# A Mamba block and a routed FFN on one core: x_proj rows split later, expert units in other slots, last part reordered, conv in slot 2 and delta's matmul in slot 3

## The reference

```python
# mixer: hidden = ctx (4, 1024, 512), z = layernorm(x) over (B, DI, L)
x  = einsum('ed,bld->bel', in_proj_w, hidden)
u  = silu(causal depthwise conv, 4 taps, of x + conv_b)
x_dbl = einsum('ke,bel->bkl', x_proj_w, u)        # 32 rows dt, 16 B, 16 C
delta = softplus(dt_proj_w @ dt + dt_proj_b)
state = state * exp(delta * A) + (delta * u) * B_t   # 16 states per channel, scan over time
y  = (sum over states of state * C_t + D * u) * silu(z)
x1 = x + y^T
# FFN: on xn = layernorm(x1)
logits = xn.reshape(4, -1) @ switch_w.T + switch_b   # 8 experts, top 2 per batch row
h = gelu(xh @ w1[top]^T + b1);  o = sum_k gate_k * (h @ w2[top]^T + b2)   # 16 heads of 64
out = x1 + (xn + o) @ w3.T + b3
```

## Time and profile before

| | |
|---|---|
| median of three runs | 2472.0 us (2468.28 to 2475.02) |
| profiled execution, its own time | 2471.16 us |
| its span | 2469.3 us |
| mean granted PE clock | 0.90 of full |
| busy: DVE, PE, ACT, POOL | 86%, 82%, 65%, 59% |
| set-up ahead of the first scan | 78.9 us |
| pass 0, passes 1 to 3 (first scan to first scan) | 483 us; 584, 582 and about 545 us |
| last part, from the last scan | about 197 us |

### The profile page before, as it was taken

How to read it: one execution, slowest core, us unless ns; L and a number is a source line. 1 busy time by engine, 2 the same in 40 slices (tenths; PEclk the granted TensorE clock), 3 DMA queues, 4 the chain that set the end, 5 groups by cost and what they waited for, 6 DMA issues and landing times.

```text
span 2469.3 us, 32717 instructions
## 1 busy us (share of the span) xinstructions
PE 2013.5 (82%) x10776; PEld 1203.1 (49%) x10776; DVE 2133.6 (86%) x2712; ACT 1602.4 (65%) x2357; POOL 1445.2 (59%) x993
## 2 busy tenths in 40 slices
PE   6798888985757997996675897898685798797899
PEld 2677676653433553454453454454453455344344
DVE  5899789979999899998999899998999899999322
ACT  2677787656669868655667878855576857954500
POOL 0588677767756566566675566665775666665000
PEclk9899889997878998997888999899787899999899
DMA  5311434555612754566542464466460174578412
GB/s 174 128 37 52 150 99 148 188 162 169 246 37 103 261 166 133 161 204 203 188 155 74 140 232 152 147 224 199 154 239 26 60 253 145 164 251 283 168 56 72
DMA packets 200329, 383.01 MB, mean 155 GB/s; under 512 B 31553, under 2 KB 97089, under 8 KB 200162
## 3 DMA queue, kind: packets, MB, share of 16 engines
q1 hardware_dynamic: 196992, 380.47, 46.1%
q10 hardware_dynamic: 3170, 0.47, 0.1%
HBM read 346.80 MB, written 34.08 MB: 154 GB/s over the span
## 4 chain that ended last, share of the span: by engine, by line
PE 44%; DVE 19%; issue 17%; ACT 14%; POOL 3%; DMA 1%; DVEq 0%; SPq 0%; ACTq 0%; POOLq 0%
PE dense L1135 13%; PE dense L962 9%; DVE h L1525 9%; PE dense L900 5%; ACT dA L1246 4%; PE dense L948 3%; DVE dense L1501 3%; POOL h L865 3%; DVE u L1357 2%; PE dense L912 2%; PE dense L1112 2%; ACT L1213 2%; PE dense L921 2%; PE dense L1065 2%; PE dense L969 2%
## 5 line engine op out<-in xcount | busy, mean ns | idle before, releaser
L865 POOL TENSOR_TENSOR h<-h,Cb 128x1024 f32<-128x1024 f32 x512 | 1208.4, 2361 | 431.8 <-DVE h L1525 408.2
L1246 ACT ACTIVATE dA<-delta,Av 128x512 f32<-128x512 f32 x1024 | 703.1, 717 | 384.6 <-DVE h L1525 381.3
L962 PE MATMUL dense<-ident,h 128*128 128x128 f32 x4096 | 605.4, 299 | 165.0 <-POOL h L865 163.5
L962 PEld LDWEIGHTS dense<-ident,h 128*128 128x128 f32 x4096 | 521.1, 155 | 315.6 <-POOL h L865 225.8
L1525 DVE TENSOR_TENSOR_SCAN h<-dA,state,dense 128x512 f32<-128x512 f32 x512 | 627.4, 1263 | 31.0 <-issue 14.4
L1525 DVE TENSOR_TENSOR_SCAN h<-dA,dense 128x512 f32<-128x512 f32 x512 | 596.7, 1203 | 22.0 <-PE dense L962 8.5
L1501 DVE TENSOR_TENSOR dense<-dense,Bb 128x512 f32<-128x512 f32 x864 | 550.5, 682 | 1.6
L1135 PE MATMUL dense<-w3h,xT 128*128 128x512 f32 x832 | 386.0, 598 | 0.0
L859 POOL COPY state<-h 128x2 f32<-128x2 f32 x256 | 47.6, 186 | 336.6 <-DVE h L1525 335.1
L948 PE MATMUL dense<-Bb,duT 128*128 128x128 f32 x1280 | 179.9, 289 | 41.1 <-DVE h L1525 31.7
L1135 PEld LDWEIGHTS dense<-w3h,xT 128*128 128x128 f32 x832 | 147.9, 192 | 130.1 <-issue 130.1
(11 more groups left out here) (168 smaller groups left out, 2084.1 us busy)
## 6 DMA issues: line engine op xcount, KB each, us to landing
sww<-in_sw SPq DMA_DIRECT2D x167, 512.0 KB, 4.2
Cb<-bc_scratch SPq DMA_DIRECT2D x64, 512.0 KB, 6.1
Bb<-bc_scratch SPq DMA_DIRECT2D x54, 512.0 KB, 4.6
w3h<-in_sw SPq DMA_DIRECT2D x52, 512.0 KB, 8.2
w3h<-in_w3T SPq DMA_DIRECT2D x52, 512.0 KB, 5.2
row<-x_scratch SPq DMA_DIRECT2D x40, 512.0 KB, 4.5
xz<-in_x SPq DMA_DIRECT2D x64, 256.0 KB, 4.7
xt<-in_x SPq DMA_DIRECT2D x64, 256.0 KB, 3.9
```

The costliest lines, as they stand in the source:

```text
L865: e.tensor_tensor(h[:, s:s + 2, :], h[:, s:s + 2, :], Cb[:, 2 * q:2 * q + 2, :], ALU.mult).then_inc(prod_done, 1)
L962: mm = e.matmul(yT[:, k, :], h[:, 2 * ((PAIRS * g + q) % RH) + i, k * P:(k + 1) * P], ident[:], is_transpose=True, start=False, stop=(q == ...
L1246: e.activation(dA[:, i % RA, :], delta[:, st % 2, :], ACT.Exp, scale=Av[:, j * N + n:j * N + n + 1]).then_inc(dA_done, 1)
```

## The change

Seven edits:

- `conv_slot` is 2 for every step, so the conv stands in slot 2 and v in slot 3 in all of them, as they did where j = 7.
- `split_rows` moves on ACT behind the first dA pair, the copy of duT and uD; szT's Silu goes ahead of u's in slot 6; x_proj's first half waits for the first half of u only; the transposes of du (pass 0) go from the end of slot 7 to slot 6.
- All expert units, and the tiles behind them, start one slot later (40, 57, 84 and 100 instead of 39, 56, 83 and 99; the tiles have 22 and 27 slots instead of 23 and 28).
- The first norm's rstd and shift for the next pass go from slots 124 and 126 to 69 and 71, with two copies of their results.
- tile_out is always two slots behind its last part, in the next pass if need be.
- late_row's loads go to slot 125, and the weight loads of slots 124 and 125 behind them to 126; the four renorms of the last part go to slots 33, 35, 46 and 46.
- In the last part POOL makes the second selection of w1 (a new item, `select`) by halving adds, hidden waits only for the two w1 selections, gelu and expert_out for all of them.

```diff
 def conv_slot(st):
-    return 2 if st % J == J - 1 else 1
+    return 2
...
     def add(self, b, t, *what):
+        if b < NB and t >= STEPS * SLOTS:
+            b, t = b + 1, t - STEPS * SLOTS
         self.slots[b][t].append(what)
...
-            self.add(b, 124, "ln1_rstd")
-            self.add(b, 126, "ln1_shift")
+            self.add(b, 69, "ln1_rstd")
+            self.add(b, 71, "ln1_shift")
...
-        for u, hidden, tiles, span in ((0, 39, 56, 23), (1, 83, 99, 28)):
+        for u, hidden, tiles, span in ((0, 40, 57, 22), (1, 84, 100, 27)):
...
-                    self.add(b, at[m + W3C - 1] + 2 if at[m + W3C - 1] < 126 else 127, "tile_out", u, dh, k)
+                    self.add(b, at[m + W3C - 1] + 2, "tile_out", b, u, dh, k)
...
+        for k in range(TB):
+            self.add(b - 1, 125, "late_row", k)
         for q in range(PAIRS):
-            self.add(b - 1, 120 + q, "sw_tail", AFTER_B + q)
-            self.add(b - 1 if q < PAIRS - 1 else b, (121 + q) % 128, "sw_tail", AFTER_B + PAIRS + q)
+            for t, m in ((120 + q, q), (121 + q, PAIRS + q)):
+                t = t if t < 124 else max(t, 126)
+                self.add(b - (t < 128), t % 128, "sw_tail", AFTER_B + m)
...
-            self.add(b, 10 + SWL * k + 8, "renorm", k)
+            self.add(b, (33, 35, 46, 46)[k], "renorm", k)
...
+        self.add(b, 45, "select")
...
+                    elif what == "select":
+                        e.wait_ge(top_step, 1 + 9 * (b - 1) + 8)
+                        e.wait_ge(experts_loaded, 1 + 64 * b)
+                        e.tensor_tensor(wt1, w12[:, 0], hot[:, 1, :].unsqueeze(2).broadcast_to([P, E, HD]), ALU.mult) \
+                            .then_inc(w1_step, 1)
+                        for n, rest in ((1, 4), (2, 2)):
+                            e.wait_ge(w1_step, 1 + n)
+                            e.tensor_tensor(wt1[:, 0:rest], wt1[:, 0:rest], wt1[:, rest:2 * rest], ALU.add).then_inc(w1_step, 1)
+                        e.wait_ge(w1_step, 1 + 3)
+                        e.tensor_tensor(w1s[:, 1, :], wt1[:, 0], wt1[:, 1], ALU.add).then_inc(w1_step, 1)
...
-                e.wait_ge(u_done, 1 + J * (c + 1))
+                e.wait_ge(u_done, 1 + J * c + J // 2)
...
+                    if q == SLOTS - 2 and g + 1 < STEPS:
+                        turn_du(g + 1)
...
-                if b == 0 and q == SLOTS - 1 and g + 1 < STEPS:
-                    turn_du(g + 1)
...
-                if b < NB and late(b, t, 0) and st % J == J - 1 and c + 1 < NB * TH:
-                    split_rows(c + 1)
...
                         e.activation(uD[:], u[:, g % UR, :], ACT.Copy, scale=Dv[:, j:j + 1]).then_inc(uD_done, 1)
+                        if st % J == J - 1 and c + 1 < NB * TH:
+                            split_rows(c + 1)
```

More of the change, by code:

```diff
@@ L26 @@
 HL = DC - 1
+SELECT = 9
 SD = 128
@@ L172, in tail @@
                 self.add(b - 1, 114, "sw_tail", m)
+        for k in range(TB):
+            self.add(b - 1, 125, "late_row", k)
         for q in range(PAIRS):
-            self.add(b - 1, 120 + q, "sw_tail", AFTER_B + q)
-            self.add(b - 1 if q < PAIRS - 1 else b, (121 + q) % 128, "sw_tail", AFTER_B + PAIRS + q)
+            for t, m in ((120 + q, q), (121 + q, PAIRS + q)):
+                t = t if t < 124 else max(t, 126)
+                self.add(b - (t < 128), t % 128, "sw_tail", AFTER_B + m)
         for m in range(AFTER_B + 2 * PAIRS, SWL * TB):
             self.add(b, 0, "sw_tail", m)
-        for k in range(TB):
-            self.add(b - 1, 126, "late_row", k)
         for k in range(TB):
@@ L219, in tail @@
                         self.add(b, t, "tile", u, dh, k, c)
-                    self.add(b, t, "tile_out", u, dh, k)
+                    self.add(b, t, "tile_out", b, u, dh, k)
                     t += 4
@@ L319, in build @@
         mv1 = sb("mv1", [P, J, 2])
-        r1 = sb("r1", [P, J])
-        nm1 = sb("nm1", [P, J])
+        r1 = sb("r1", [P, 2, J])
+        nm1 = sb("nm1", [P, 2, J])
         row = sb("row", [P, 2, DI])
@@ L368, in build @@
         xT_tail = u[:, UR - J:UR, :]
-        wt = sww[:, 0].rearrange("p e s -> p (e s)")[:, 0:E * HD].rearrange("p (e f) -> p e f", e=E)
+        wt, wt1 = [sww[:, 0].rearrange("p e s -> p (e s)")[:, i * E * HD:(i + 1) * E * HD].rearrange("p (e f) -> p e f", e=E)
+                   for i in (0, 1)]
         dense = ctx.enter_context(nc.psum_tensor("dense", [P, 8, T], F32))
@@ L549, in hs_of, with selected @@
             return hs_tail if b == NB and hp % 2 else hs[:]
+        def selected(b):
+            return SELECT * (b - 1) if b <= NB else SELECT * NB - 2
         def part_index(b, uu, dh, k, c):
@@ L779, in slot @@
                     elif what == "tile_out":
-                        uu, dh, k = a
-                        n = part_index(b, uu, dh, k, 0) // W3C
+                        fb, uu, dh, k = a
+                        n = part_index(fb, uu, dh, k, 0) // W3C
                         lo = half(uu) * T + k * P
-                        e.wait_ge(evac[bank_of(b, "tile", uu, dh, k)], 1 + count(b, "tile", uu, dh, k) + 1)
-                        e.dma_start(out[b - 1:b, lo:lo + P, dh * QD:(dh + 1) * QD]
+                        e.wait_ge(evac[bank_of(fb, "tile", uu, dh, k)], 1 + count(fb, "tile", uu, dh, k) + 1)
+                        e.dma_start(out[fb - 1:fb, lo:lo + P, dh * QD:(dh + 1) * QD]
                                     .rearrange("o p d -> p (o d)"), res[:, n % 2]).then_inc(out_stored[n % 2], 16)
@@ L1047, in slot @@
                         if hp == 0:
-                            e.wait_ge(sel_step, 1 + 9 * b)
+                            e.wait_ge(sel_step, 1 + selected(b) + (5 if b < NB else 3))
+                            if b == NB:
+                                e.wait_ge(w1_step, 1 + 4)
                             for i in (0, 1):
@@ L1059, in slot @@
                         bank = bank_of(b, *name)
+                        if hp == 0:
+                            e.wait_ge(sel_step, 1 + selected(b + 1))
                         for i in (0, 1):
@@ L1260, in slot @@
                         e.wait_ge(xz_loaded, 1 + 16 * (g + 1))
-                        e.activation(xz[:], xz[:], ACT.Identity, scale=r1[:, j:j + 1], bias=nm1[:, j:j + 1]) \
+                        e.activation(xz[:], xz[:], ACT.Identity, scale=r1[:, b % 2, j:j + 1], bias=nm1[:, b % 2, j:j + 1]) \
                             .then_inc(zn_done, 1)
@@ L1271, in slot @@
                         e.wait_ge(x1_done, 1 + g)
+                        e.wait_ge(zT_done, 1 + g + 1)
+                        e.activation(szT[:].rearrange("p k e -> p (k e)"), dense[:, S, :], ACT.Silu) \
+                            .then_inc(evac[S], 1)
                         if g == 0:
@@ L1276, in slot @@
                             silu_u(G, S, last_step(b, st, "in_proj"))
-                        e.wait_ge(zT_done, 1 + g + 1)
-                        e.activation(szT[:].rearrange("p k e -> p (k e)"), dense[:, S, :], ACT.Silu) \
-                            .then_inc(evac[S], 1)
                         exp_ln_table()
@@ L1365, in ln1_shift @@
                 e.wait_ge(ln1_rs, 1 + b + 1)
-                e.scalar_tensor_tensor(out=nm1[:], in0=mv1[:, :, 0], scalar=-1.0 / (DI if b else 1), in1=r1[:], op0=ALU.mult,
+                e.scalar_tensor_tensor(out=nm1[:, b % 2], in0=mv1[:, :, 0], scalar=-1.0 / (DI if b else 1), in1=r1[:, b % 2], op0=ALU.mult,
                                        op1=ALU.mult).then_inc(ln1_done, 1)
@@ L1587, in route2 @@
                 done = 1
-                for src, on, dst in ((w12[:, 0], hot[:, 0, :], w1s[:, 0, :]), (w12[:, 0], hot[:, 1, :], w1s[:, 1, :]),
-                                     (w12[:, 1], hot[:, 3, :], w2s[:])):
+                first = [(w12[:, 0], hot[:, i, :], w1s[:, i, :]) for i in ((0,) if b == NB else (0, 1))]
+                for src, on, dst in (*first, (w12[:, 1], hot[:, 3, :], w2s[:])):
                     e.wait_ge(sel_step, 1 + n + done)
@@ L1597, in route2 @@
                                        b1s[:]).then_inc(sel_step, 1)
-                e.wait_ge(sel_step, 1 + n + 8)
+                e.wait_ge(sel_step, 1 + n + done + 1)
                 e.tensor_tensor_reduce(lgm[:, :, 0], b2c[:], rt[:, 4, :], 1.0, 0.0, ALU.mult, ALU.add,
                                        b2s[:]).then_inc(sel_step, 1)
-                e.wait_ge(sel_step, 1 + n + 9)
+                e.wait_ge(sel_step, 1 + n + done + 2)
             turns(slot)
```

27 lines of the change are left out of this document (14 added, 13 removed).

## The result

The changed kernel takes 2524.5 us (median of four runs, 2522.75 to 2525.46) against 2470.5 (four runs): 1.0217 times, 95% interval 1.0201 to 1.0233. Forecast were 2475 and a range of 2455 to 2495, so the prediction was wrong by 50 us. The profiled execution took 2524.9 us, its span 2523.0.

What follows compares the result with a forecast made beforehand. The scan loop was taken as bound by DVE, the last part by PE. Terms 20 + 16 - 1.4 - 2.4 - 10.7 - 4.8 - 1.5 - 7 - 4.3 = +3.9 us on 2471.2 gave 2475, range 2455 to 2495.

Steps and rivals of the forecast that it cites:

- the new waits: Pass 0, 14 further steps: delta waits for v behind PE's product of state 9, 3.65 us each, 51 us.
- the credit against them: Pass 0, same 14 steps: present idle gaps of 30.7 us set against the new waits, net +20 us.
- my upper bound of 40: Pass 0, conv edit: net +20 us, bounds +14 and +40, the latter by a clock that is always low.
- Why delta waits: Pass 0: PE makes state 9's product ahead of v, and that product waits for the scan of state 6.
- Conv, passes 1 to 3: Steps ahead of tiles +8 us, tile steps with v late on PE +8, tap waits outside expert steps -1.4.
- Split of x_proj's rows: Steps 7 and 15: -1.2 us each, -2.4; steps 31 and 47: stall returns at delta, 0.
- Expert slots: Passes 1 to 3: steps 23, 39, 55 save -10.7 us at v and -4.8 in front; other expert steps -1.5.
- Norm and tile_out: Ends of passes: POOL waits of 5.4 us and tile_out's last-slot waits go, 9.0 us, less possible lag: -7.
- The last part: After the scan loop: waits for late_row, renorms in ACT's queue and weight selections shrink, -4.3 us.
- The first, a lower clock on v: Rival, chance 0.20: PE's lower clock sits on v in most steps, pass 0 up to 40 us; 2493, slower.
- The third rival: Expert steps: gelus in slots 3 and 7 hold DVE 1 us more over some 12 steps; 2487, slower; chance 0.10.
- The second: Rival, chance 0.20: delta's wait 2.8 us a step, pass 0 costs 8, chunk ends give 8 more; 2455, faster.

Runs made afterwards that it cites:

- the rest: All of the change except the conv and expert-slot edits, against the kernel before: 2435.2 us, 0.9862.
- v ahead: Changed kernel, conv still in slot 2, PE in pass 0 making v ahead of the sum of pair 1 and the product of state 9: 2478.1 us, 1.0033.
- V ahead of the tiles: The 2478.1 us kernel, with v in passes 1 to 3 also ahead of slot 2's tile parts and logits, one slot earlier: 2462.1 us, 0.9972.
- The run two slots later: The change without its conv edit, expert units and tiles two slots later than in the kernel before (41, 58, 85, 101): 2442.9 us, 0.9890.
- both undone: The changed kernel with the conv and the expert units back in their old slots: 2435.2 us, 0.9862 against the kernel before.

## Why the prediction was wrong, point by point

Along one path the sum is now: 2470.2, the rest -35.0, expert slots +20.5, conv +68.8, which makes 2524.5. Forecast were about -14, -17 and +34.6. The shares hang on the order: beside the conv's edit the expert slots cost 9.9 us, and the conv alone cost 74.2. By place, the forecast's terms add up to some +14 us in pass 0, -6 in passes 1 to 3 and -4 in the last part; measured are +37.0, +21.9 and -6.5. So two steps failed, of about equal weight: in pass 0 the idle time that was set against delta's new waits, and in passes 1 to 3 the sign of the expert slots.

**Conv, pass 0: the new waits right, the credit against them wrong.** For 14 steps I took 51 us of waits for delta; added up over these steps in the changed kernel they are 51.2. The step that failed is "Against it go the idle gaps that these 14 steps have now ... 30.7 us", with its reason, that "a pause in mid-step lets POOL and PE make up". Beside delta's waits these steps hold 23.9 us of idle time, over three quarters of the old sum. The taps' 15.2 us did go, but the scans' waits for PE's sums, which the pause was to take away, rose from 8.2 to 17.9 us. In steps 1 to 6 the scan of state 12 waits 1.93 us for PE, because the pause stopped PE too, through the products that wait for scans, and PE came back with its queue still in order and at a lower clock. So the edit alone cost 46.7 us in pass 0, above my upper bound of 40, and 59.7 on top of the others. Part of that difference is the transposes' edit, which removes the taps' gaps without the conv's help. With the conv in slot 2 it seems to have nothing left to give: from the edit alone to the whole change pass 0 fell by 9.7 us, about what the split gives; no run moved the transposes back beside the conv. I credited a gap to one edit that another edit of the same change removes for nothing. That moves some 15 us from one price to the other and is not why the whole came out high.

**Why delta waits** was right: v's place in PE's queue. With v ahead and the conv still in slot 2, pass 0 fell by 49.4 us. What is left against the conv in slot 1 (470.4 against 460.1) is 10 us, for the lost cover and for all else that the later slot brings; no run separates these.

**Conv, passes 1 to 3: mechanism right, size not one number.** Forecast were 14.6 us. The edit alone cost 29.1 (6.5, 9.0, 13.7), with all other edits but the expert slots 18.2, and in the whole change 8.1. It is mainly the tile steps: in pass 3 the changed kernel waits 3.2, 3.5 and 2.7 us at delta in steps 57, 60 and 61, where none or 0.7 stood before. I had counted 1 to 2 us for two of these and left 60 out. V ahead of the tiles saves 16 us here, but 13.5 with the conv in slot 1 as well, so that is a gain of its own and not the conv's price given back.

**Split of x_proj's rows: sign right, size off.** -2.4 forecast, -9.0 measured. Right were the steps of passes 1 and 2, where nothing comes out, and the 3.1 us before scan 2 in step 7. Wrong were the 1.2 us a step, where 4.1 stay won, and that szT "will wait longer": in the changed kernel it waits 3.74 us (3.76 before).

```profile
296.54 2.33 DVE L1551 TENSOR_TENSOR_SCAN h<-dA,dense 128x512 f32<-128x512 f32 x2 [3.13 <-ACT dA L1270]
302.60 0.69 DVE L1451 TENSOR_TENSOR szT<-dense,szT 128x512 f32<-128x512 f32 x1 [3.74 <-PE dense L983]
```

**Transposes of du a slot earlier: a term left out.** I counted it only as part of the split, in two steps. It acts in most steps of pass 0 and is worth 14 to 15 us, the largest gain of a single edit among those tried. The row that told it was in the trace of step 5 before, and I had looked for the tap's releaser no further than ACT:

```profile
210.76 0.58 ACT L1209 COPY duT<-dense 128x512 f32<-128x512 f32 x1 [0.95 <-PE dense L929]
```

**Expert slots: wrong sign.** -17 forecast (-10.7 - 4.8 - 1.5), +9.9 measured beside the conv, +20.5 without. This is the second step that failed. Delta's wait in step 23 did fall, from 3.46 to 1.22, but in step 55 only from 3.79 to 3.29. With the conv in slot 1 the new slots raise out_add's waits in passes 1 to 3 from 14.7 to 32.9 us and delta's from 23.0 to 37.0, and take only some 7 us of taps' waits away. The forecast has no term for out_add's, though their row stood in the trace before. What I missed is seen just before step 22 of the changed kernel:

```profile
798.47 5.60 PE L921 MATMUL dense<-ctxs,win 128*128 128x512 f32 x8 [0.24 <-ACT szT L1299]
...
804.00 1.13 PE L1080 MATMUL dense<-xT,w1s 64*128 64x512 f32 x4
...
805.20 1.28 ACT L1357 ACT_TABLE_LOAD   x1 [2.33 <-PE dense L1080]
806.50 1.26 ACT L1357 ACTIVATE hs<-dense,small 128x512 f32<-128x512 f32 x2
...
807.86 1.08 PE L1092 MATMUL dense<-hs,w2s 128*64 128x512 f32 x4 [1.71 <-ACT hs L1357]
...
808.98 0.75 DVE L1503 SCALAR_TENSOR_TENSOR xT<-dense,small,xT 128x512 f32<-128x512 f32 x1 [3.37 <-PE dense L1092]
```

The units' hidden now falls into slot 6, behind in_proj (5.6 us of PE). Gelu, expert_out and out_add follow in a chain of 5 us, and out_add is first in the next step on DVE. In the old slots hidden stood in slot 5, in front of in_proj, and in slot 7, with out_add in slot 1. I had followed the gelus on ACT, and neither hidden on PE nor out_add on DVE; I wrote for steps 23, 39 and 55 that "the last unit's out_add is now first in the step", as a reason why their stall stays, and did not ask the same of the other units. The run two slots later supports this: the waits in step 21 go. It does not separate hidden's place from gelu's in slot 3 (delta waited 1.9 us there in steps 21 and 22).

**Norm and tile_out: half right.** The norm's waits fell from 5.4 to 0.4 us. Tile_out's did not go: in step 31 it waits 3.81 us (2.52 before), in step 47 5.20 (1.09 before).

```profile
1149.85 0.69 DVE L1515 TENSOR_TENSOR res<-dense,res 128x512 f32<-128x512 f32 x1 [3.81 <-PE dense L1161]
```

With x_proj's earlier first half these edits are what is left of the rest, 35.0 - 14.5 - 9.0 - 6.0 = 5.5 us; they were not tried one by one.

**The last part: near.** -4.3 forecast, -6.5 in the change and -6.0 with both undone (197.0 to 191.1). The waits that it named are gone in the changed kernel, 4.0 us of the late statistics and 2.92 of the first hidden (0.2 are left). But with the transposes' edit alone, which touches nothing there, the last part took 194.1 us, so the size is not shown to within 3 us.

**The rivals.** The first, a lower clock on v, is not what happened: in pass 0 v took 1.12 to 1.22 us in 14 of 16 steps, and 2.07 in steps 11 and 12. But the lower clock fell on other work. PE's granted clock in pass 0 went from 0.95 to 0.91, and the same 2928 matmuls kept PE busy 445.4 us instead of 423.9. In step 5 it fell behind both of PE's pauses, on the three things ahead of v and on those ahead of the sum that the scan of state 12 needs. For the first wait that cost about 0.5 us (3.72 against 3.21 in steps 13 and 15, at full clock), for the second about 1.6 us: from the four matmuls at 249.43 to the end of the sum behind them are 4.00 us, and the same three groups took 2.37 in step 5 before. Together that is an estimate of 2.1 us a step, 13 in steps 1 to 6, of the 37 us of the pass. With v ahead the granted clock is 0.94 and PE busy 427.3 us, so that run does not separate the queue from the clock that goes with it. The Trainium skill, TensorE: Matmul & The Clock Gate, A second HAM failure mode: psum-queue depth-cycling, says that frequent short idling between groups makes the clock swing, at a cost in throughput. The trace agrees. The third rival (expert units lose) was true, with a size beyond what I gave it. The second had its gains at the ends of the chunks about right (8 us, and the split alone gave 9.0), but not its cheap wait: it had 2.8 us a step, and 51.2 us over 14 steps are 3.7.
